# A post-norm decoder layer on one core: x loaded first, weight set-up spread over the first batches, bf16 sums and new step orders

## The chip, the cores and the metric

One core of a Trainium2 chip runs the kernel. The metric is device time in microseconds of one execution. TensorE does matmuls (PE, its weight loads are PEld), VectorE is DVE, ScalarE is ACT, GpSimd is POOL, and SyncE's queue (SP) issues all transfers of this kernel.

## The reference

For each of 64 batches, with 128 tokens of 512 features:

```
qkv = x @ Wqkv; q, k = rmsnorm(q) * w, rmsnorm(k) * w; 16 heads of 32; rope
x = layernorm(x + softmax(causal(q k^T / sqrt(32))) v @ Wo)
# cross step on x and ctx, both cut by tokens into 8 heads of 16 rows:
#   q = x rows (16 x 512), k = v = ctx rows (16 x 512)
#   scores 512 x 512 = q^T k / 4; softmax; out (16 x 512)
x = layernorm(x + cross(x, ctx))
# ffn: x and weight (512 x 512) rounded to fp8 e4m3 in blocks of 128, scaled back
x = layernorm(x + x_deq @ w_deq.T)
```

## The kernel before

All five engines run one software pipeline over the batches. A batch passes through stages 0 to 8; in a slot t an engine works on stage s of batch t − s. Each engine has its list (SP_STEPS, POOL_STEPS, ACT_STEPS, DVE_STEPS, PE_STEPS) of words like `ffn:2@7`: step ffn, part 2, stage 7. It goes through its list in order once per slot, skipping batches that do not exist; slots 0 to 10 are written out, then 25 rounds of two slots are a loop, then the rest is written out. A step waits on semaphores for what it needs, so a step that waits holds all behind it on its engine. The list is cyclic: what counts is the order round the slot. Where it is cut, and so the stage number of a step, only names the turn.

The products are split for accuracy: a value is a high half in f16 and a low half in f16, and a projection of one 128-row part is three matmuls of 128x512 (split); Wo uses fp32r halves (linear).

What passes in one batch:

- SP loads x (ld_x). ACT squares it (x_square), TensorE sums the squares over partitions with a matrix of ones, plus a tiny value (x_sum, two fp32 matmuls of one column), DVE makes a power-of-two scale (x_exp) and from it vinv. POOL and ACT make the halves xs (x_scale, x_high, x_low), SP turns them by a DMA transpose (turn_x).
- TensorE projects q, k, v (proj_q, proj_k, proj_v). q and k go through squares, rms, rope_terms, rope_sum, part_high and part_low, and SP turns each by a DMA transpose (turn_parts:0 and :1, line 414) into qs and ks.
- Self scores come in two turns: self_scores for the maxima (self_max), whose negatives become two more rows of qs by way of DRAM (self_shift, st_sh1, ld_sh1), then self_scores_T, exp (self_probs), mask, self_pv, self_recip, self_norm, oT_high and oT_low, proj_o, add_self, layer norm 0 (layer_mean, layer_devs, layer_rstd, layernorm). x2 is stored.
- The context is loaded (ld_cx, into the one buffer cx, which context_T of the batch before must have read), scaled and split (ctx_square, ctx_sum as x_sum, ctx_exp, context_high, context_low), and turned by TensorE (context_T). q rows and k rows go to DRAM and back in a cross layout (st_qpl, st_kpl, ld_qp, ld_kp).
- 16 cross_scores, each a pair of matmuls on 64-row tiles into the one tile mx, each read by a cross_max on DVE (line 811, 128x1024); then cross_shift, st_sh2, ld_sh2; 16 cross_scores_T into the one tile st, each read by an exp on ACT (probs, line 645) into pp; 8 cross_pv, 32-column tiles; cross_turn, cross_scale, add_cross, layer norm 1.
- The fp8 rounding: quant_scale and quant_magic (DVE), quant_unit and quant_round (POOL), then the halves xd (xd_high, xd_low), their DMA transpose turn_xd (line 465), four ffn parts (line 983), add_ffn, layer norm 2, st_out.

Each full-bank product takes a bank of a fixed three by turn. cross_shift, its rows' store and load must be through before cross_scores_T:0.

Ahead of the lists stands the set-up. SP loads wqkv, wffn, wo and then x's first batch; ACT squares wqkv and wffn; DVE and TensorE make the weight scales (u_wsc); ACT and DVE make w_h and w_l, wo_h and wo_l; then DVE quantises each of the four blocks of the ffn weights, TensorE turns it and DVE splits it (wf_h, wf_l). Only after u_done do ACT, POOL and TensorE go into their lists.

Of the kernel before, what the change touches and what calls it, by code (L numbers as in the profile page):

```python
# [5 lines left out]
def post_ln_decoder_kernel(nc, x, ctx_in, wqkv, q_norm_w, k_norm_w, wo, wffn, cos_t, sin_t, out):  # L6
# [43 lines left out]
    with es:  # L50
# [141 lines left out]
        POOL_STEPS = steps("""  # L192
            ctx_scale:0@4 layer_rstd:0@3 layer_mean:2@8 context_low:0@4 layer_rstd:2@8 layer_mean:1@7
            mean_square:0@1 layer_rstd:1@7 rope_sum:0@1 mean_square:1@1 part_low:0@1 quant_unit:0@7
            mask:0@2 mask:1@2 rope_sum:1@1 mask:2@2 mask:3@2 cross_scale:0@6 quant_round:0@7
            query_low:0@3 part_low:1@1 oT_low:0@2 quant_round:1@7 quant_round:2@7 xd_low:0@7
            x_scale:0@0 x_low:0@0 cross_scale:1@6 layer_mean:0@2""")
        ACT_STEPS = steps("""
            probs:8@6 layernorm:0@3 square:0@1 layer_devs:1@7 probs:9@6 layernorm:1@7 probs:10@6
            square:1@1 part_high:0@1 self_probs:0@2 probs:11@6 query_high:0@3 value:0@1  # L200
            self_probs:1@2 probs:12@6 x_square:0@0 self_probs:2@2 probs:13@6 self_probs:3@2
            part_high:1@1 probs:14@6 probs:15@6 oT_high:0@2 probs:0@5 context_out:0@4 probs:1@5
            ctx_square:0@3 xd_high:0@7 probs:2@5 x_high:0@0 probs:3@5 probs:4@5 layer_devs:0@2
            probs:5@5 context_high:0@3 probs:6@5 layer_devs:2@7 probs:7@5 layernorm:2@7""")
        DVE_STEPS = steps("""
            self_shift:0@2 cross_max:12@5 rope_terms:0@1 cross_max:13@5 quant_scale:0@7
            cross_max:14@5 cross_max:15@5 rope_terms:1@1 cross_shift:0@5 cross_max:0@4 cross_turn:0@6
            cross_max:1@4 quant_magic:0@7 cross_max:2@4 self_recip:0@2 self_norm:0@2 cross_max:3@4
            x_exp:0@0 cross_max:4@4 cross_turn:1@6 cross_max:5@4 add_self:0@2 cross_max:6@4
            self_max:0@1 ctx_exp:0@3 self_max:1@1 cross_max:7@4 self_max:2@1 cross_max:8@4  # L210
            ctx_inv:0@4 add_ffn:0@7 cross_max:9@4 self_max:3@1 cross_max:10@4 add_cross:0@6
            cross_max:11@4""")
        PE_STEPS = steps("""
            cross_scores_T:10@6 proj_k:2@1 proj_k:3@1 cross_scores:14@5 proj_v:0@1 proj_v:1@1
            self_scores_T:0@2 cross_scores_T:11@6 cross_scores:15@5 proj_v:2@1 proj_v:3@1
            self_scores_T:1@2 cross_scores_T:12@6 cross_scores:0@4 cross_pv:3@6 self_pv:0@2
            self_scores_T:2@2 cross_scores_T:13@6 self_pv:1@2 cross_scores:1@4 self_scores_T:3@2
            cross_pv:4@6 self_pv:2@2 cross_scores:2@4 cross_scores_T:14@6 self_pv:3@2 cross_pv:5@6
            cross_scores_T:15@6 cross_scores:3@4 cross_pv:6@6 context_T:0@4 cross_scores_T:0@5
            x_sum:0@0 cross_pv:7@6 cross_scores:4@4 cross_scores_T:1@5 proj_o:0@2 proj_o:1@2  # L220
            cross_scores:5@4 cross_scores_T:2@5 proj_o:2@2 proj_o:3@2 cross_scores:6@4
            cross_scores_T:3@5 self_scores:0@1 self_scores:1@1 ctx_sum:0@3 cross_pv:0@5
            cross_scores:7@4 cross_scores_T:4@5 self_scores:2@1 ffn:0@7 ffn:1@7 cross_scores_T:5@5
            cross_scores:8@4 ffn:2@7 ffn:3@7 cross_scores_T:6@5 cross_scores:9@4 proj_q:0@0
            self_scores:3@1 cross_scores_T:7@5 cross_scores:10@4 proj_q:1@0 proj_q:2@0
            cross_scores_T:8@5 cross_scores:11@4 proj_q:3@0 proj_k:0@0 proj_k:1@0 cross_scores:12@4
            cross_scores_T:9@5 cross_pv:1@5 cross_pv:2@5 cross_scores:13@4""")
# [924 lines left out]
```

## Time and profile before

| | |
|---|---|
| median of 3 runs | 2737.21 us (2735.64 to 2741.36) |
| profiled execution, its time | 2741.84 us |
| its span, first to last instruction | 2740.1 us |
| mean granted TensorE clock | 0.971 |
| busy: PE, DVE, ACT, POOL | 91%, 80%, 76%, 61% |
| chain that ended last: PE, SP queue, DMA | 65%, 11%, 9% |

Starts and durations in a timeline are in us from the span's start. PE durations overlap, since matmuls are pipelined; the distance from one start to the next is the price.

### The profile page before, as it was taken

The numbers are of one execution on the slowest core, as the hardware profiler recorded it, in microseconds if no ns is written. First come the engines' busy times: TensorE is split into PE (matmuls) and PEld (weight loads), VectorE is DVE, ScalarE is ACT, GpSimd is POOL, SyncE is SP. The second block draws the span as 40 slices with busy tenths as digits, with TensorE's granted clock in tenths as the row PEclk, the third lists the DMA queues.
The fourth block names the chain that finished last, engine by engine and source line by source line (L and its number), as shares of the span: only waits on it lengthen the run. The fifth ranks groups of instructions, "written<-read, shape, count | busy, mean of one in ns | idle before, by whom it ended". The sixth has DMA issues, their size and how long they took to land.

```text
span 2740.1 us, 67073 instructions
## 1 busy us (share of the span) xinstructions
PE 2488.1 (91%) x19220; PEld 992.2 (36%) x19220; DVE 2203.3 (80%) x3525; ACT 2074.7 (76%) x3097; POOL 1670.0 (61%) x2586
## 2 busy tenths in 40 slices
PE   0679999999999999999999999999999999998874
PEld 0333333343334333333333333433333333433211
...
GB/s 88 66 103 121 119 125 114 129 123 121 119 129 119 128 112 131 121 128 112 127 128 125 115 119 132 123 118 122 128 119 123 117 131 120 130 115 115 71 41 28
DMA packets 610637, 312.01 MB, mean 114 GB/s; under 512 B 469504, under 2 KB 551424, under 8 KB 610560
## 3 DMA queue, kind: packets, MB, share of 16 engines
...
q8 instruction: 39, 0.64, 0.1%
q14 instruction: 38, 0.31, 0.0%
...
## 4 chain that ended last, share of the span: by engine, by line
PE 65%; SPq 11%; DMA 9%; issue 5%; DVE 5%; POOL 3%; ACT 2%; ACTq 0%; POOLq 0%; DVEq 0%
PE bank L983 25%; PE pv L1112 13%; PE mx L1085 8%; PE st L1099 7%; DMA xdT<-xd 7%; SPq L414 5%; PE bank L1048 2%; PE bank L1030 2%; PE bank L975 2%; PE bank L1051 2%; DVE nm L811 2%; SPq L388 2%; SPq L398 1%; PE bank L968 1%; SPq L379 1%
## 5 line engine op out<-in xcount | busy, mean ns | idle before, releaser
L811 DVE TENSOR_REDUCE nm<-mx 128x2 f32<-128x1024 f32 x1024 | 1248.5, 1219 | 248.7 <-PE mx L1085 241.9
L645 ACT ACTIVATE pp<-st,esc 128x1024 f32<-128x1024 f32 x1024 | 1139.3, 1113 | 341.8 <-PE st L1099 339.1
L1112 PE MATMUL pv<-pp,vT 128*32 128x512 f32 x4096 | 550.3, 622 | 1.2 <-DVE o2t L906 0.9
L983 PE MATMUL bank<-w_h,xsT 128*128 128x512 f16 x1536 | 525.0, 384 | 9.3 <-DMA xsT<-xs 6.3
L1085 PE MATMUL mx<-kp,qp 48*128 48x512 f16 x2048 | 400.7, 388 | 36.9 <-DVE nm L811 34.4
L1099 PE MATMUL st<-qp,kp 50*128 50x512 f16 x2048 | 401.2, 388 | 25.0 <-ACT pp L645 25.0
L983 PE MATMUL bank<-w_l,xsT 128*128 128x512 f16 x768 | 293.0, 381 | 0.0
L983 PE MATMUL bank<-wf_h,xdT 128*128 128x512 f16 x512 | 180.2, 394 | 83.2 <-DMA xdT<-xd 83.1
L983 PEld LDWEIGHTS bank<-w_h,xsT 128*128 128x128 f16 x1536 | 150.1, 98 | 278.2 <-issue 131.1
L534 POOL TENSOR_SCALAR neg_mean<-total 128x1 f32<-128x1 f32 x192 | 36.5, 190 | 329.3 <-DVE yout L938 207.2
L558 POOL TENSOR_SCALAR_AFFINE_SELECT p<-p 128x512 f32<-128x512 f32 x256 | 168.3, 657 | 108.1 <-ACT p L695 103.1
L1085 PEld LDWEIGHTS mx<-kp,qp 48*128 48x128 f16 x2048 | 99.4, 94 | 354.9 <-DVE nm L811 229.4
L872 DVE SCALAR_TENSOR_TENSOR rope<-bank,rms,rope_w 128x1024 f32<-128x1024 f32 x128 | 163.4, 1277 | 37.6 <-POOL rms L514 19.9
L841 DVE TENSOR_REDUCE nm<-bank 128x4 f32<-128x512 f32 x256 | 174.6, 683 | 14.9 <-PE bank L1020 14.9
L1099 PEld LDWEIGHTS st<-qp,kp 50*128 50x128 f16 x2048 | 99.5, 94 | 219.4 <-ACT pp L645 120.9
L695 ACT ACTIVATE p<-bank 128x512 f32<-128x512 f32 x256 | 156.1, 610 | 24.2 <-PE bank L1030 24.1
L511 POOL TENSOR_SCALAR rms<-ssq,xeps 128x1 f32<-128x1 f32 x128 | 33.9, 265 | 192.6 <-ACT junk L669 192.4
L552 POOL TENSOR_TENSOR qkn<-rope,qkn 128x512 f16<-128x512 f32 x128 | 148.0, 1156 | 3.2 <-ACT qkn L676 3.2
L1112 PEld LDWEIGHTS pv<-pp,vT 128*32 128x32 f32 x4096 | 93.6, 110 | 141.4 <-issue 131.8
L711 ACT ACTIVATE x<-x,shift,rstd 128x512 f32<-128x512 f32 x128 | 103.3, 807 | 48.5 <-POOL shift L543 48.5
L975 PE MATMUL bank<-wo_h,oT_h 128*128 128x512 f32 x256 | 116.7, 456 | 6.6 <-POOL oT_l L574 6.6
L539 POOL TENSOR_SCALAR rstd<-devs 128x1 f32<-128x1 f32 x192 | 36.6, 190 | 133.6 <-ACT junkd L706 123.2
...
## 6 DMA issues: line engine op xcount, KB each, us to landing
qp<-q_rows SPq DMA_DIRECT2D x256, 96.0 KB, 2.3
kp<-k_rows SPq DMA_DIRECT2D x256, 96.0 KB, 2.2
...
```

Source lines behind the costliest of these rows:

```text
L552: g_.tensor_tensor(qkn[k][:, :, 2 - k, :], rope[:, 0].rearrange("p h a d -> p h (a d)"), qkn[k][:, :, 0, :], ALU.subtract).then_inc(s_part ...
L558: g_.affine_select(out=p1[c % 2][:], in_=p1[c % 2][:], compare_op=ALU.is_ge, fill=0.0, base=0, pattern=[[0, HC], [1, P]], channel_multipli ...
L645: a.activation(pp[:, unit % PB, 2 * l:2 * (l + 1), :], st[:], ACT.Exp, scale=esc[b.i][:])\
L695: a.activation(p1[c % 2][:], at(f"s1t{c}")[:].rearrange("p (h q) -> p h q", h=HC), ACT.Exp, scale=SELF_SCALE).then_inc(bank_free[BANK[f"s1 ...
L811: v.tensor_reduce(cols, mx[:], AX.X, ALU.max, negate=True).then_inc(mx_free, 1)
L841: v.tensor_reduce(nm1[:, HC * c:HC * (c + 1)], at(f"s1m{c}")[:].rearrange("p (h k) -> p h k", h=HC), AX.X, ALU.max, negate=True).then_inc( ...
L872: v.scalar_tensor_tensor(rope[:].rearrange("p t h a d -> p t (h a d)"), at("qk"[k])[:].unsqueeze(1).to_broadcast([P, 2, D]), rms[:, k:k + ...
L975: last = t.matmul(at(name)[:], a[:, rows], w[:, part, cols], start=(part == 0 and i == 0), stop=(part == KC - 1 and i == 2))
L983: last = t.matmul(at(name)[:], lin[:, KC * lo + part, :], w[:, part, cols], start=(part == 0 and i == 0), stop=(part == KC - 1 and i == 2))
L1085: last = t.matmul(mx[:, q, :], qp[b.i][rows, p, c * P:(c + 1) * P], kp[b.i][rows, p, :], start=True, stop=True)
L1099: last = t.matmul(st[:, q, :], kp[b.i][rows, p, i * P:(i + 1) * P], qp[b.i][rows, p, :], start=True, stop=True)
L1112: last = t.matmul(pv[32 * j:32 * j + 2 * XD, :], vT[b.i][:, i, GROUPS * j + g, :], pp[:, unit % PB, j, :], start=(i == 0), stop=(i == KC - 1))
```

## The change

- **Set-up.** ld_x of batch 0 goes first on SP, then the loads of wqkv and wffn. Functions of the set-up are hooked ahead of or behind steps of given batches (ahead, behind in run): qkv_high, qkv_low and qkv_scale make the q, k, v weights after the first x_high, x_exp and ahead of the first proj_q; fixed_rows (POOL's memsets of qkn, vT and kp) after the weight scale; load_wo, wo_high, wo_low ahead of turn_parts:0, self_probs:0, self_recip of batch 0; wf_halves(0) ahead of the first self_max, (1) to (3) ahead of add_self of batches 0, 1, 2.
- **ffn weights.** wf_halves writes the halves of a block into xd, and SP turns it by a DMA transpose (turn_wf) into wf; the ffn matmuls read their moving operand as four pieces of 128 columns.
- **Sums.** ones and tiny are bf16; x_sum, ctx_sum and the weights' sum read the upper 16 bits of the fp32 squares as bf16.
- **Small moves.** xeps goes from x_scale to behind x_low; vinv from x_exp to behind rope_terms:0.
- **Orders.** All five lists are new; the steps are the same.

```diff
         SP_STEPS = steps("""
-            ld_kp:1@5 st_qpl:0@4 ld_qp:1@5 turn_xd:0@8 turn_x:0@1 ld_x2r:0@7 ld_qp:0@4 ld_x:0@0
-            st_out:0@8 st_sh1:0@2 st_kpl:0@4 ld_sh1:0@2 ld_kp:0@4 st_sh2:0@5 st_x2:0@3 ld_xr:0@2
-            ld_sh2:0@5 turn_parts:0@1 ld_cx:0@3 turn_parts:1@1""")
+            st_sh2:0@5 ld_x:0@0 ld_sh2:0@5 turn_parts:0@1 turn_parts:1@1 ld_qp:1@4 ld_kp:1@4
+            ld_cx:0@3 turn_xd:0@7 st_qpl:0@3 turn_x:0@0 ld_x2r:0@6 ld_qp:0@3 st_kpl:0@3 st_sh1:0@1
+            st_out:0@7 ld_sh1:0@1 ld_kp:0@3 st_x2:0@2 ld_xr:0@1""")
         POOL_STEPS = steps("""
...
+            context_low:0@4 layer_mean:0@3 layer_mean:2@8 cross_scale:1@7 layer_rstd:2@8
+            layer_rstd:0@3 mean_square:0@1 layer_mean:1@7 layer_rstd:1@7 rope_sum:0@1 mean_square:1@1
+            mask:0@2 part_low:0@1 mask:1@2 quant_unit:0@7 rope_sum:1@1 mask:2@2 mask:3@2 part_low:1@1
+            quant_round:0@7 quant_round:1@7 oT_low:0@2 quant_round:2@7 xd_low:0@7 x_scale:0@0
+            cross_scale:0@6 query_low:0@3 x_low:0@0 ctx_scale:0@3""")
         DVE_STEPS = steps("""
...
+            add_self:0@3 self_max:1@2 cross_max:7@5 ctx_exp:0@4 cross_max:8@5 self_max:2@2
+            cross_max:9@5 add_ffn:0@8 self_max:3@2 cross_max:10@5 self_shift:0@2 cross_max:11@5
+            add_cross:0@7 cross_max:12@5 rope_terms:0@1 cross_max:13@5 cross_max:14@5 quant_scale:0@7
+            ctx_inv:0@5 cross_max:15@5 cross_shift:0@5 cross_max:0@4 rope_terms:1@1 cross_max:1@4
+            cross_turn:0@6 quant_magic:0@7 cross_max:2@4 self_recip:0@2 self_norm:0@2 cross_max:3@4
+            x_exp:0@0 cross_max:4@4 cross_max:5@4 cross_turn:1@6 cross_max:6@4 self_max:0@1""")
         PE_STEPS = steps("""
...
+            cross_scores_T:10@6 cross_scores:12@5 proj_k:0@1 cross_pv:1@6 cross_pv:2@6
+            cross_scores:13@5 proj_k:1@1 proj_k:2@1 cross_scores_T:11@6 cross_scores:14@5 proj_k:3@1
+            self_scores_T:0@2 proj_v:0@1 cross_scores_T:12@6 cross_scores:15@5 proj_v:1@1 proj_v:2@1
+            cross_scores_T:13@6 cross_scores:0@4 self_scores_T:1@2 proj_v:3@1 cross_pv:3@6
+            cross_scores_T:14@6 cross_scores:1@4 self_pv:0@2 self_scores_T:2@2 self_pv:1@2
+            cross_scores_T:15@6 self_scores_T:3@2 cross_scores:2@4 cross_pv:4@6 self_pv:2@2
+            self_pv:3@2 cross_pv:5@6 cross_scores_T:0@5 cross_scores:3@4 cross_pv:6@6 x_sum:0@0
+            cross_scores_T:1@5 cross_pv:7@6 cross_scores:4@4 cross_scores_T:2@5 context_T:0@4
+            proj_o:0@2 cross_scores:5@4 cross_scores_T:3@5 proj_o:1@2 proj_o:2@2 cross_scores:6@4
+            cross_scores_T:4@5 self_scores:0@1 proj_o:3@2 self_scores:1@1 cross_scores_T:5@5
+            cross_scores:7@4 cross_pv:0@5 ctx_sum:0@3 ffn:0@7 cross_scores_T:6@5 cross_scores:8@4
+            ffn:1@7 self_scores:2@1 cross_scores_T:7@5 cross_scores:9@4 ffn:2@7 ffn:3@7
+            self_scores:3@1 cross_scores_T:8@5 cross_scores:10@4 proj_q:0@0 proj_q:1@0
+            cross_scores_T:9@5 cross_scores:11@4 proj_q:2@0 proj_q:3@0""")
...
+            def load_weights():
+                for c in range(KC):
+                    sp.dma_start(pp[:, c].rearrange("p a d -> p (a d)")[:, 0:3 * D], wqkv[c * P:(c + 1) * P, :])\
+                      .then_inc(d_setup[c], 16)
+                for c in range(KC):
+                    sp.dma_start(wf_rows[c][:], wffn[c * P:(c + 1) * P, :]).then_inc(d_wffn, 16)
...
+            def turn_wf(c):
+                sp.wait_ge(u_wf, c + 1)
+                sp.dma_start_transpose(wf[:, c], xd[:].rearrange("p a d -> p (a d)")).then_inc(d_wf, 16)
...
+            def fixed_rows():
+                pool.wait_ge(u_wsc, 1)
+                for n, (rows, value) in enumerate([(qkn[0][:, :, 3, :], 0.0), (qkn[1][:, :, 3, :], SHIFT_UNIT)] + [
+                        (vT[i][:, :, :, XD:2 * XD], 1.0) for i in range(2)] + [
+                        (kp[i][ROW_TILE * q + 32:ROW_TILE * (q + 1), :, :], SHIFT_UNIT) for i in range(2) for q in range(2)]):
+                    pool.wait_ge(u_const, U_FIRST + n)
+                    g_.memset(rows, value).then_inc(u_const, 1)
+                pool.wait_ge(u_const, U_CONST)
...
+            def wf_halves(c):
+                y3 = yq[:].rearrange("p (n k) -> p n k", n=NQ)
                 src = wf_rows[c][:].rearrange("p (n k) -> p n k", n=NQ)
...
+                if c:
+                    dve.wait_ge(d_wf, 16 * c)
+                step(v.tensor_copy(xd[:, 0, :], yq[:]))
+                v.tensor_tensor(xd[:, 1, :], yq[:], xd[:, 0, :], ALU.subtract).then_inc(u_wf, 1)
...
-                t.matmul(at("xt")[:, 0:1], ones[:], xss[:], start=True, stop=False)
-                t.matmul(at("xt")[:, 0:1], ones[:], tiny[:], start=False, stop=True).then_inc(bank_full[BANK["xt"]], 1)
+                t.matmul(at("xt")[:, 0:1], ones[:], xss[:].bitcast(BF16)[:, 1:2], start=True, stop=False)
+                t.matmul(at("xt")[:, 0:1], ones[:], tiny[:, 0:1], start=False, stop=True).then_inc(bank_full[BANK["xt"]], 1)
...
-                split("ffn", xdT, wf_h, wf_l, slice(0, D), part)
+                for i, (lo, w_lo) in enumerate(((0, 0), (0, 1), (1, 0))):
+                    last = t.matmul(at("ffn")[:].rearrange("p (c n) -> p c n", c=KC), xdT[:, KC * lo + part, :],
+                                    wf[:, :, KC * w_lo + part, :], start=(part == 0 and i == 0),
+                                    stop=(part == KC - 1 and i == 2))
```

The four old lists besides SP's are the kernel's own above. POOL's ended `... rope_sum:1@1 mask:2@2 mask:3@2 cross_scale:0@6 quant_round:0@7 query_low:0@3 part_low:1@1 oT_low:0@2 quant_round:1@7 quant_round:2@7 xd_low:0@7 ...`, and DVE's had cross_max:14 and :15 side by side and no other two.

## Rows read from the trace of the kernel before

**Rows 1.** Windows: length, busy time (instructions) per engine, PEclk, DMA share, GB/s.

```profile
0.00:75.15 75.15, 6.43 (x24) 4.72 (x25) 38.71 (x72) 20.09 (x28) 13.66 (x29) 1.00 0.24 85
75.15:301.00 225.85, 181.98 (x1343) 85.81 (x1345) 134.08 (x212) 116.34 (x197) 114.08 (x172) 0.91 0.44 101
...
600.00:2152.00 1552.00, 1510.17 (x11978) 607.76 (x11976) 1347.84 (x2160) 1280.15 (x1920) 1034.62 (x1599) 1.00 0.49 123
```

**Rows 2.** The line of the v scale, batches 8 to 63 (window 300 to 2600 us).

```profile
L866 DVE TENSOR_SCALAR vinv<-sx,wtop x56: 212/214/215, 326.5 to 2467.1; 128x1 int32<-128x1 int32 x56
```

**Rows 3.** Timeline of the set-up: start, duration, instruction, [idle before <- releaser].

```profile
3.58 7.37 POOL L497 MEMSET kp<- 32x2048 f16 x4
...
10.31 0.42 DVE L761 SCALAR_TENSOR_TENSOR rope_w<-rope,sin_s 128x256 f32<-128x256 f32 x1
...
24.52 7.00 DVE L777 SCALAR_TENSOR_TENSOR w_l<-pp,wsc,w_h 128x1536 f16<-128x1536 f32 x4 [1.64 <-ACT w_h L634]
...
35.48 0.68 DVE L789 TENSOR_REDUCE amax<-x 128x4 f32<-128x512 f32 x1
...
39.97 0.69 DVE L798 TENSOR_TENSOR yq<-yq,qsc 128x512 f32<-128x512 f32 x1
...
67.01 0.63 ACT L658 ACTIVATE junkx<-xb 128x512 bf16<-128x512 f32 x1 [32.18 <-DVE amax L805]
...
75.15 0.61 PE L983 MATMUL bank<-w_h,xsT 128*128 128x512 f16 x1 [6.33 <-DMA xsT<-xs]
```

**Rows 4.** Waits from 600 to 2152 us: us in total, times, longest.

```profile
PE bank L983 <- DMA xdT<-xd: 40.4, 40, 1.5
...
DVE nm L811 <- PE mx L1085: 124.2, 120, 2.2
```

**Rows 5.** Chain of waits, one batch: start, duration, piece.

```profile
1300.60 0.60 PE bank L968 x4
...
1302.13 3.06 SPq L414
...
1309.17 3.38 DMA xdT<-xd
```

**Rows 6.** Timeline of POOL and of SP's queue in that batch.

```profile
1306.23 1.16 POOL L603 TENSOR_TENSOR xd<-yq,xd 128x512 f16<-128x512 f32 x1 [0.88 <-ACT xd L732]
...
1295.58 2.92 SPq L443 DMA_DIRECT2D qp<-cross_shift  x4
```

**Rows 7.** Timeline of TensorE in that batch.

```profile
1277.05 0.38 PE L1085 MATMUL mx<-kp,qp 48*128 48x512 f16 x2
1277.36 0.39 PE L983 MATMUL bank<-w_h,xsT 128*128 128x512 f16 x1
...
1301.43 0.38 PE L991 MATMUL bank<-xss,ones 128*128 128x1 f32 x2
...
1301.97 1.06 PE L1112 MATMUL pv<-pp,vT 128*32 128x512 f32 x8
...
1308.23 0.38 PE L1017 MATMUL bank<-maskb,identb 128*128 128x512 bf16 x1
1308.45 0.39 PE L1020 MATMUL bank<-ks,qs 96*128 96x128 f16 x4
1308.67 0.34 PE L1073 MATMUL bank<-css,ones 128*128 128x1 f32 x2
...
1309.16 1.06 PE L1112 MATMUL pv<-pp,vT 128*32 128x512 f32 x8
```

**Rows 8.** A group of lines (busy, mean ns), then DVE's timeline in that batch.

```profile
L1017 PEld LDWEIGHTS bank<-maskb,identb 128*128 128x128 bf16 x256 | 24.9, 97 | 71.1 <-issue 61.3 <-DVE nm L841 1.8 <-DVE cbits L827 0.9
...
1290.22 1.23 DVE L811 TENSOR_REDUCE nm<-mx 128x2 f32<-128x1024 f32 x1 [0.64 <-PE mx L1085]
...
1293.08 0.24 DVE L822 STREAM_TRANSPOSE sh2T<-sh 128x64 f16<-128x64 f16 x1
```

**Rows 9.** Waits from 75 to 290 us: us in total, times, longest.

```profile
DVE x L899 <- PE bank L975: 15.0, 5, 6.7
```

**Rows 10.** Timeline of DVE in the fill.

```profile
98.33 0.69 DVE L841 TENSOR_REDUCE nm<-bank 128x4 f32<-128x512 f32 x1 [9.00 <-PE bank L1020]
```

More of the change, by code:

```diff
@@ L192, in post_ln_decoder_kernel @@
         POOL_STEPS = steps("""
[L193 to L197, printed above, removed]
-        ACT_STEPS = steps("""
[L199 to L204, printed above, removed]
@@ L205, in post_ln_decoder_kernel @@
-        DVE_STEPS = steps("""
[L206 to L212, printed above, removed]
@@ L213, in post_ln_decoder_kernel @@
-        PE_STEPS = steps("""
[L214 to L227, printed above, removed]
@@ L309, in last_of, with run @@
                     for i in sorted({p.bank for p in points})]
-        def run(eng, table, fns):
+        def run(eng, table, fns, ahead, behind):
             def slot(t, rnd=None):
@@ L315, in slot @@
                     if 0 <= t - stage < BATCH:
+                        if (name, k, t) in begins:
+                            ahead[begins[name, k, t]]()
                         fns[name](Count(t - stage, rnd), k)
+                        if (name, k, t) in ends:
+                            behind[ends[name, k, t]]()
+            stage_of = {(name, k): stage for name, k, stage in table}
+            begins = {(name, k, stage_of[name, k] + b): (name, k, b) for name, k, b in ahead}
+            ends = {(name, k, stage_of[name, k] + b): (name, k, b) for name, k, b in behind}
             for t in range(LOOP0):
@@ L492, in _ @@
             n = 4
[L493 to L495 removed]
+            for rows, value in [(ones[:], 1.0), (tiny[:], TINY), (sums_of[:], 0.0)]:
                 pool.wait_ge(u_const, n)
@@ L614, in _ @@
                 "part_low": part_low, "mask": mask,
-                "context_low": context_low, "xd_low": xd_low, "cross_scale": cross_scale, "oT_low": oT_low, "quant_unit": quant_unit, "quant_round": quant_round, "query_low": query_low})
+                "context_low": context_low, "xd_low": xd_low, "cross_scale": cross_scale, "oT_low": oT_low, "quant_unit": quant_unit, "quant_round": quant_round, "query_low": query_low},
+                ahead={("mean_square", 0, 0): fixed_rows}, behind={})
         @block.scalar
@@ L947, in _ @@
                 "cross_turn": cross_turn, "add_cross": add_cross, "quant_scale": quant_scale,
-                "quant_magic": quant_magic, "add_ffn": add_ffn})
+                "quant_magic": quant_magic, "add_ffn": add_ffn}, ahead={
+                    ("self_max", 0, 0): lambda: wf_halves(0), ("self_recip", 0, 0): wo_low,
+                    ("add_self", 0, 0): lambda: wf_halves(1), ("add_self", 0, 1): lambda: wf_halves(2),
+                    ("add_self", 0, 2): lambda: wf_halves(3)},
+                behind={("x_exp", 0, 0): qkv_low})
         @block.tensor
@@ L1126, in _ @@
                 "cross_scores": cross_scores, "ctx_sum": ctx_sum,
-                "cross_scores_T": cross_scores_T, "cross_pv": cross_pv, "ffn": ffn})
+                "cross_scores_T": cross_scores_T, "cross_pv": cross_pv, "ffn": ffn}, ahead={
+                    ("proj_q", 0, 0): qkv_scale, ("proj_o", 0, 0): wo_ready, ("ffn", 0, 0): wf_ready}, behind={})
 def kernel(x, ctx_2048, L0_attn_Wqkv, L0_attn_q_norm_w, L0_attn_k_norm_w, L0_attn_Wo, L0_ffn_weight):
```

183 lines of the change are left out of this document (94 added, 89 removed).

## The prediction

> **What bounds the kernel now.** I read the windows by stage first [rows 1]. There the reader is to see the stages. In the first 75 us TensorE does 6.4 us of work while DVE sets up weights. From 75 to 301 us the pipeline fills. Between 600 and 2152 us everything repeats: by the first and last of the rows of the v scale [rows 2] batches 8 to 63 follow one another every (2467.1 − 326.5)/55 = 38.92 us, and the forty batches of the 1552 us window every 38.8 us. After the last v scale at 2467 the pipeline drains for 273 us.
>
> Set-up next [rows 3]. The q, k, v weights are ready when DVE's four w_l passes end, at 31.5 us. After that DVE quantises and turns the ffn weights, four rounds of about 7.85 us (35.48 to 67.0), and only then may ACT square the first x (idle before it 32.2 us) and the first projection start, at 75.15. Nothing in the first projection needs the ffn weights: 75.15 − 31.5 = 43.6 us is order alone.
>
> In the steady state TensorE is busy 1510 of 1552 us, and the waits there [rows 4] have one entry for its matmuls: the turned xd, 40.4 us in 40 times, 1.0 us a batch. The DVE waits for scores, 124.2/40 = 3.1 us a batch, are idle time of an engine that has some. The chain [rows 5] shows why xdT is late. It leaves TensorE at the context transpose (1300.60), goes to the SP queue, where the load of cx waited for it, then through the 3.06 us that turning k holds the queue, two kp loads, the q stores, two qp loads, and issues the transpose of xd at 1309.17, 8.0 us after the context was turned; it lands 3.38 us later and ffn starts. xd itself was complete on POOL at 1306.23 + 1.16 = 1307.39 [rows 6]: the queue, not the data, was last, by 1.8 us. So a batch costs 37.8 us of TensorE's own order and 1.0 us for the SP queue's order.
>
> **The change, part by part.** *Sums over partitions.* The two fp32 matmuls on the squares of x and the two on those of the context take 1301.97 − 1301.43 = 0.54 us and 1309.16 − 1308.67 = 0.49 us [rows 7], 1.03 us a batch, each fp32 matmul being two instructions (x2 in the rows). In bf16 they are four instructions with a load of 97 ns (24.9 us in 256, [rows 8]). The bound below is the pitch of the 128-column f16 matmuls, 128x512 columns' worth in 0.22 us for four (1308.45 to 1308.67), so 0.22 for the four together; the bound above is half of today's, 0.52, since half the instructions go. I take 0.42, close to four loads of 97 ns, because a one-column matmul can hide no load: 0.6 us saved a batch, 0.5 to 0.8.
>
> The row of bf16 loads stands at 97 ns [rows 8]. [...]
>
> *New order on TensorE.* The same 75 steps. Inside a run of full-array matmuls the pitch is 0.22 us; where the order goes over to the 64-row pairs of the cross scores and back it is 0.31 (1277.05 to 1277.36) [rows 7]: a change of tile shape costs 0.09 us. Counted round the list, the order before has 41 such changes, the new one 42: +0.1 us. The Trainium skill says on the page "TensorEngine Tiling (Array Packing)", section "Key Properties", that changing the tiling mode drains the engine; it names no price, and by its rule too the new order is the dearer one, by one drain. The trace agrees and prices it.
>
> *New order on SP.* ld_cx is now followed at once by turn_xd; turn_parts:1 and the loads of the second halves stand ahead of ld_cx, the q store and loads behind. From the end of context_T the path to ffn is now the issue of cx, which took less than 0.9 us with its semaphores (1301.20 to 1302.13, rows 5), and a 3.4 us transpose, some 4.3 us. Adding up the TensorE steps between context_T and ffn:0 in the new list (four proj_o at 0.71, two self_scores at 0.44, six cross steps at 0.22, one cross_pv at 0.88, the sum, nine shape changes) gives 6.8 us. That link has 2.5 us to spare; before it was 11.4 against some 10. What is late next: POOL's xd_low. Its new list puts query_low and cross_scale:0 (each about as long as the 1.16 us of xd_low or less) behind xd_low and lets nothing new in front, so against the scores it ends about 1 to 2 us sooner than the 1307.39 of today, which was already early. After that come the two transposes of q and k, now back to back. The second must leave the queue (3.06 us), then four loads (0.4 us each at the transfers' pace of rows 6) and ld_cx, before turn_xd; laid beside the TensorE list, part_low:1 ends about 7.8 us after cross_scores:0, so turn_xd goes at about 14 to 15, lands at 17.4 to 18.5, and ffn:0 stands at 18.9. Room of 0.4 to 1.5 us: I cost the wait at 0, with 1.0 as its other end.
>
> *New orders on DVE, ACT, POOL.* DVE is busy 33.7 us of 38.8 (1347.84/40, rows 1). A cross_max can't start before its scores and the next scores not before it ends, so where two stand side by side DVE idles 0.64 us (1290.22, [rows 8]). The new list has two such pairs for one of before, and x_exp gives up the 0.3 us of vinv. DVE then needs some 35.5 us of a batch; a batch of 37.3 still covers it, but with 1.8 us to spare instead of 3.3. Before moves nothing for it. The mean bound: TensorE loses 0 to 0.6 us a batch where a cross_max is late.
>
> So a batch goes from 38.8 to 38.8 − 1.0 − 0.6 + 0.1 = 37.3 us, and over 55 batches that is 55 × 1.5 = 82 us (bounds 36.9 and 38.2: 104 and 33 us).
>
> *Set-up.* SP loads x first (under 0.5 us of queue), then the weights. ACT squares x, and DVE's x_exp comes behind its rope tables, which end at about 10.7; x_high ends about 1 us later [rows 3]. ACT then starts the squares of the weights some 2 us later than before, of which most was waiting for data; with the queue's 0.5 I take 0.8 us for the whole chain: the weight scale, known 1.64 us before the first w_l at 24.52, comes at 23.7, and w_l ends near 32.3. POOL's four memsets of kp (7.37 us) and the four smaller ones (an eighth to a quarter of its data each, taken as 2.2 in all) are moved behind the weight scale: they end at 33.3, and TensorE, ACT and SP all wait for them. First projection at about 33.5 instead of 75.15: 41.7 us saved. Bounds: 38 (everything of x in line with the weights' squares, 2 us more, and slower loads) and 43.6.
>
> *What set-up costs later.* Each of the four wf_halves is the DVE round of before, 5.2 us from 35.48 to 39.97 + 0.69 [rows 3], plus a copy and a subtraction of 0.69 each, 6.6 us in all; their transposes go by SP, half as many columns each as that of k. wo adds four passes at 0.69 on DVE and as many on ACT. That is 29 us of DVE in the fill, where it is busy 134 of 226 us [rows 1]. The first round stands before the first self_max, where DVE idled 9.0 us for the turned k (98.33, [rows 10]): hidden. The others stand before add_self, where DVE idled 15.0 us in 5 times, 3 us each [rows 9]: 6.6 − 3 = 3.6 us late, three times. Taken as all exposed with wo it would be 3 × 6.6 + 5 = 25 us, and 0 if the slots are bound elsewhere. I take 8. The ffn matmuls read the weights in four pieces of 128 columns at a stride; the nearest row, the mask matmul with its repeated 128-column piece, keeps the full pitch (1308.23 to 1308.45), so 0. The drain keeps its steps: 0, within ±8.
>
> **The sum.** The profiled execution took 2741.84 us (span 2740.1 and 1.7 around it). 2741.84 − 41.7 + 8 − 82 = 2626. The median of the runs is 4.6 us below that execution, so 2621; I say 2620.
>
> **The rivals.** *A, as summed: 2620*, its own range 2590 to 2650. *B, the SP queue or POOL still brings xdT last.* For it: the two transposes stand together, and the room is only 0.4 to 1.5 us. Against it: the 8.0 us between context and issue falls to about 0.7. Then only the sums' 0.5 us remains: 2737 − 34 − 28 = 2675, and with nothing left of it 2703. *C, DVE takes the bound.* For it: 35.5 of 37.3 us and two adjacent pairs. Period 37.9: 2737 − 34 − 50 = 2653. *D, slower: the shift rows come too late for cross_scores_T:0.* In the trace sh2T is made at 1293.08 [rows 8] and the last of four issues on SP is out at 1298.5 [rows 6]; even if it lands 2 us after its start that is about 6.7 us after the shift; the new list gives 7.6 us from the shift to cross_scores_T:0. DVE would have to run more than 0.9 us late for any wait; it decides at a wait of 1.5 + 34/55 = 2.1 us a batch, that is with cross_shift 3 us late. At 2.5 us a batch the time is 2737 − 34 + 55 = 2758. Against it: DVE had 3.3 us of idle time a batch for its waits [rows 4], and catches up. *E, better: 2575*, TensorE's sums at 0.22 us and small waits gone too (period 36.6).
>
> **How the numbers follow.** A 0.50, B 0.22, C 0.13, D 0.05, E 0.10. The range 2585 to 2695 leaves out half of E (0.05), a third of B (0.07) and D (0.05). A measurement of this kernel can tell about 0.2%, 5.5 us. Faster 0.94 (all but D and a sliver), same 0.01, slower 0.05.
>
> **What would show it.** First projection near 33.5 us; no DVE round of the ffn weights ahead of it. Batches 8 to 63 at 37.3 us by the rows of vinv. No entry of TensorE for xdT in the steady waits; bf16 rows of the sums with two instructions a step. DVE busy about 33.7 of 37.3. B shows as an xdT wait with SP's turn_parts in the chain, C as cross score matmuls waiting for nm, D as st matmuls waiting for cross_shift. A first projection later than 45 us, a period above 38.2, or a fill (first projection to batch 8) longer by more than 25 us than 251 us would prove the sum wrong.

## The result and the profile after

The changed kernel takes **2624.08 us** (median of 3 runs, 2621.92 to 2624.45) where the kernel before takes 2737.21: a ratio of 0.9582, with a 95% interval of 0.956 to 0.9603. The forecast was 2620, the range 2585 to 2695. The profiled execution took 2624.45 us with a span of 2622.7. Its page, busy time and the chain that ended last:

```profile
PE 2448.5 (93%) x18946; PEld 932.2 (36%) x18946; DVE 2204.5 (84%) x3524; ACT 2096.8 (80%) x3097; POOL 1686.3 (64%) x2586
...
PE 87%; DVE 4%; issue 2%; POOL 2%; ACT 2%; DMA 2%; SPq 0%; POOLq 0%; DVEq 0%; ACTq 0%
```

In the kernel before, TensorE had 65% of the chain and SP's queue 11%; now TensorE has 87% and the queue nothing. The windows of the fill and of the steady state (columns as in [rows 1]):

```profile
33.00:260.00 227.00, 160.01 (x1067) 72.03 (x1070) 136.37 (x222) 94.05 (x163) 93.65 (x139) 0.81 0.41 93
600.00:2152.00 1552.00, 1551.86 (x12361) 596.47 (x12360) 1407.71 (x2251) 1351.21 (x2000) 1089.16 (x1663) 1.00 0.51 128
```

TensorE is busy 1551.86 of 1552 us (its ends are modelled), where it was 1510.17 [rows 1], and its list of waits from 600 to 2152 us is empty: the 40.4 us for xdT [rows 4] have no successor. DVE still waits for scores, though less than the 124.2 us of [rows 4]:

```profile
DVE nm L842 <- PE mx L1126: 90.0, 168, 0.7
```

DVE needs 1407.71/1552 of the time, 33.8 us of a batch of 37.2.

To divide the gain I take one marker in both traces, the transpose sh2T on DVE, once a batch. Before: batch 8 at 516.54 us, then 38.906 us a batch. After, batches 8 and 63:

```profile
492.61 0.24 DVE L853 STREAM_TRANSPOSE sh2T<-sh 128x64 f16<-128x64 f16 x1
...
2540.09 0.24 DVE L853 STREAM_TRANSPOSE sh2T<-sh 128x64 f16<-128x64 f16 x1
```

That is (2540.09 − 492.61)/55 = 37.227 us a batch. The difference of the spans, 2740.1 − 2622.7 = 117.4 us, splits so:

| part | before | after | gained |
|---|---|---|---|
| first projection at | 75.15 | 32.88 | 42.3 |
| from there to sh2T of batch 8 | 441.4 | 459.7 | −18.3 |
| 55 batches at | 38.906 | 37.227 | 92.4 |
| from sh2T of batch 63 to the end | 83.7 | 82.6 | 1.1 |

The 38.906 holds two long intervals where the drain begins, 40.65 and 43.83 us, with the granted clock at 0.89 and 0.81 (windows between the rows of sh2T):

```profile
2495.50:2536.15 40.65, 32.98 (x260) 12.17 (x260) 31.86 (x49) 29.13 (x39) 20.21 (x31) 0.89 0.45 106
2536.15:2579.98 43.83, 33.93 (x232) 11.10 (x226) 28.77 (x42) 26.33 (x34) 15.91 (x25) 0.81 0.28 73
```

Batches 8 to 58 alone follow every 38.82 us before and every 37.23 after. The changed kernel has no interval above 38.4 us.

Three more places of the after trace. **Set-up**: ACT and DVE, then POOL and TensorE (timeline as in [rows 3]):

```profile
8.67 0.63 ACT L691 ACTIVATE junkx<-xb 128x512 bf16<-128x512 f32 x1 [6.51 <-DMA xb<-x]
...
24.46 7.01 DVE L812 SCALAR_TENSOR_TENSOR w_l<-pp,wsc,w_h 128x1536 f16<-128x1536 f32 x4 [1.73 <-ACT w_h L662]
...
25.45 7.37 POOL L529 MEMSET kp<- 32x2048 f16 x4
...
32.88 0.61 PE L1024 MATMUL bank<-w_h,xsT 128*128 128x512 f16 x1 [10.91 <-POOL kp L529]
```

The projection starts 0.06 us after the memsets of kp end (25.45 + 7.37 = 32.82); the w_l passes end at 31.47, so the memsets are last by 1.35 us.

**SP's queue** in one steady batch (timeline: start, duration of the issue), and xd on POOL. xd_low ends at 1289.08 and its transpose is issued at 1289.25, so SP now waits for the data. xdT lands at 1292.31 and ffn starts at 1293.34, 1.0 us later:

```profile
1287.30 0.36 SPq L384 DMA_DIRECT2D cx<-ctx  x1
1289.25 1.24 SPq L483 DMA_TRANSPOSE xdT<-xd  x1
...
1287.92 1.16 POOL L632 TENSOR_TENSOR xd<-yq,xd 128x512 f16<-128x512 f32 x1 [0.88 <-ACT xd L767]
```

**TensorE** at the two sums of that batch (compare 1301.43 and 1308.67 in [rows 7]):

```profile
1283.95 0.18 PE L1032 MATMUL bank<-xss,ones 128*128 128x1 bf16 x1
1283.99 0.16 PE L1033 MATMUL bank<-tiny,ones 128*128 128x1 bf16 x1
1284.10 0.39 PE L1140 MATMUL st<-qp,kp 50*128 50x512 f16 x2
...
1293.27 0.18 PE L1114 MATMUL bank<-css,ones 128*128 128x1 bf16 x1
1293.31 0.16 PE L1115 MATMUL bank<-tiny,ones 128*128 128x1 bf16 x1
1293.34 0.81 PE L1162 MATMUL bank<-wf,xdT 128*128 128x512 f16 x3
```

From the start of a sum to the next matmul it is 0.15 us with a change of tile shape and 0.07 us without one: 0.22 us a batch, where the four fp32 matmuls took 1.03. The two are not quite alike, since before a change of tile shape stood behind both sums; e4 below, with the new order and fp32, makes them alike.

### The profile page after: what moved, and what is told of

Its sections match the earlier page's. It is cut to its first block, busy times and chain, and to the rows that moved or that the text cites. A ratio compares the mean times of both kernels' runs of the same rounds, so it can differ in the third digit from the quotient of the medians.

```text
span 2622.7 us, 66428 instructions
## 1 busy us (share of the span) xinstructions
PE 2448.5 (93%) x18946; PEld 932.2 (36%) x18946; DVE 2204.5 (84%) x3524; ACT 2096.8 (80%) x3097; POOL 1686.3 (64%) x2586
## 4 chain that ended last, share of the span: by engine, by line
PE 87%; DVE 4%; issue 2%; POOL 2%; ACT 2%; DMA 2%; SPq 0%; POOLq 0%; DVEq 0%; ACTq 0%
PE bank L1024 19%; PE pv L1153 18%; PE st L1140 11%; PE mx L1126 10%; PE bank L1016 7%; PE bank L1162 7%; PE bank L1089 3%; PE bank L1071 3%; PE bank L1058 2%; PE bank L1061 2%; PE bank L1092 2%; DVE nm L842 1%; PE bank L1009 1%; ACT pp L678 1%; DMA xdT<-xd 0%
## 5 line engine op out<-in xcount | busy, mean ns | idle before, releaser
L1024 PE MATMUL bank<-w_h,xsT 128*128 128x512 f16 x1536 | 547.2, 386 | 12.9 <-POOL kp L529 10.9
L1153 PE MATMUL pv<-pp,vT 128*32 128x512 f32 x4096 | 544.6, 617 | 0.4 <-DVE o2t L938 0.3
L1024 PEld LDWEIGHTS bank<-w_h,xsT 128*128 128x128 f16 x1536 | 150.6, 98 | 266.4 <-issue 132.0
L1162 PE MATMUL bank<-wf,xdT 128*128 128x512 f16 x768 | 203.2, 389 | 23.5 <-DMA xdT<-xd 23.4
L587 POOL TENSOR_SCALAR_AFFINE_SELECT p<-p 128x512 f32<-128x512 f32 x256 | 183.2, 726 | 39.0 <-ACT p L728 38.9
L899 DVE SCALAR_TENSOR_TENSOR rope<-bank,rms,rope_w 128x1024 f32<-128x1024 f32 x128 | 163.7, 1279 | 44.2 <-POOL rms L541 23.5
L702 ACT ACTIVATE junk<-bank 128x512 bf16<-128x512 f32 x128 | 76.4, 597 | 86.6 <-PE bank L1024 77.0
L593 POOL TENSOR_SCALAR cxs<-cx,sc 128x512 f32<-128x512 f32 x64 | 44.2, 690 | 136.0 <-DVE sc L862 136.0
L739 ACT ACTIVATE junkd<-x,neg_mean 128x512 bf16<-128x512 f32 x128 | 92.4, 722 | 48.0 <-POOL neg_mean L563 42.0
```

The lines of the kernel that those rows point to most:

```text
L587: g_.affine_select(out=p1[c % 2][:], in_=p1[c % 2][:], compare_op=ALU.is_ge, fill=0.0, base=0, pattern=[[0, HC], [1, P]], channel_multipli ...
L899: v.scalar_tensor_tensor(rope[:].rearrange("p t h a d -> p t (h a d)"), at("qk"[k])[:].unsqueeze(1).to_broadcast([P, 2, D]), rms[:, k:k + ...
L1024: last = t.matmul(at(name)[:], lin[:, KC * lo + part, :], w[:, part, cols], start=(part == 0 and i == 0), stop=(part == KC - 1 and i == 2))
L1153: last = t.matmul(pv[32 * j:32 * j + 2 * XD, :], vT[b.i][:, i, GROUPS * j + g, :], pp[:, unit % PB, j, :], start=(i == 0), stop=(i == KC - 1))
L1162: last = t.matmul(at("ffn")[:].rearrange("p (c n) -> p c n", c=KC), xdT[:, KC * lo + part, :], wf[:, :, KC * w_lo + part, :], start=(part ...
```

## The experiments

Eleven runs. Each ratio is to the kernel before, run again on the same chip: e1 to e4 on one chip, e5 to e8 on a second, e9 to e11 on a third. The medians of the kernel before on these three are 2732.04, 2732.51 and 2739.17 us, so times of different chips can't be compared to better than 0.3%. "us a batch" is between the sh2T of batches 8 and 63, "fill" from the first projection to the sh2T of batch 0. The last four columns are of one profiled execution each, and the fills of one kernel differ by 3 us (160.9 and 157.8).

| run | median us | ratio, 95% | first projection | fill | us a batch | span |
|---|---|---|---|---|---|---|
| kernel before | 2737.21 | 1 | 75.15 | 129.0 | 38.906 | 2740.1 |
| changed | 2624.08 | 0.9582 | 32.88 | 160.9 | 37.227 | 2622.7 |
| e1 bf16 sums only | 2753.69 | 1.0087 [1.006, 1.0114] | 73.68 | 131.1 | 39.03 | 2751.1 |
| e2 turn_xd earlier | 2701.97 | 0.9889 [0.9862, 0.9917] | 75.04 | 131.2 | 38.321 | 2701.4 |
| e3 both | 2697.66 | 0.9878 [0.9853, 0.9903] | 73.49 | 129.0 | 38.194 | 2694.2 |
| e4 orders only | 2684.14 | 0.9824 [0.9799, 0.9849] | 75.07 | 132.0 | 38.021 | 2682.3 |
| e5 old orders | 2722.51 | 0.9965 [0.9948, 0.9982] | 33.01 | 140.4 | 39.194 | 2725.5 |
| e6 rounds elsewhere | 2611.36 | 0.9561 [0.9545, 0.9577] | 32.82 | 147.9 | 37.216 | 2606.0 |
| e7 fewer shape changes | 2673.57 | 0.9788 [0.9771, 0.9806] | 32.8 | 157.2 | 38.116 | 2671.7 |
| e8 e6, e7, wo moved | 2663.65 | 0.9752 [0.9736, 0.9769] | 32.83 | 147.0 | 38.088 | 2661.6 |
| e9 rounds one slot earlier | 2607.88 | 0.9516 [0.95, 0.9532] | 32.8 | 144.9 | 37.28 | 2608.3 |
| e10 e1 with needless matmuls | 2732.63 | 0.9974 [0.996, 0.9987] | 73.58 | 128.9 | 38.789 | 2730.9 |
| e11 changed kernel again | 2623.64 | 0.9578 [0.9562, 0.9594] | 32.78 | 157.8 | 37.282 | 2620.9 |

**e1: the bf16 sums alone.** The kernel before with `ones` and `tiny` in bf16 and the high halves of the sums as operands:

```
-t.matmul(at("xt")[:, 0:1], ones[:], xss[:], start=True, stop=False)
-t.matmul(at("xt")[:, 0:1], ones[:], tiny[:], start=False, stop=True)
+t.matmul(at("xt")[:, 0:1], ones[:], xss[:].bitcast(BF16)[:, 1:2], start=True, stop=False)
+t.matmul(at("xt")[:, 0:1], ones[:], tiny[:, 0:1], start=False, stop=True)
```

> Before, with the sums over partitions in bf16 and nothing else. Additive theory (my sum): TensorE's own order gets 0.6 to 0.9 us shorter, so a batch falls from 38.9 to about 38.1 and the time by 40 to 55 us, to about 2690. Rival (the queue theory taken to its end): both sums stand between context_T and ffn in TensorE's list, and that stretch is waited out by the SP queue's path from context_T to the turned xd; then the batch stays at 38.9, the wait for xdT grows from 1.0 to about 1.8 us, and the time stays within 5 us of before.

It became 0.9% slower, which neither the sum nor the rival had. In this order both sums lie between the context transpose and ffn, inside the stretch that SP's queue waits out [rows 5], so what TensorE saves it waits. Waits of TensorE from 600 to 2152 us, against 40.4 in [rows 4]:

```profile
PE bank L984 <- DMA xdT<-xd: 67.3, 40, 2.3
```

That explains no gain, but not a loss. The loss is uneven: of the 55 batches, 10 take over 40 us, while the median batch is 38.7 us, a little below the 38.9 of before. Nine of the ten lie before the drain, where the kernel before has none. The windows of one of the ten (columns as in [rows 1], PEclk the third from the end) and its timeline on TensorE:

```profile
1355.00:1360.00 5.00, 3.65 (x34) 1.49 (x33) 4.73 (x9) 3.48 (x6) 3.85 (x7) 1.00 0.75 198
1360.00:1365.00 5.00, 4.39 (x14) 1.28 (x15) 1.07 (x2) 1.25 (x3) 0.93 (x3) 0.66 0.28 52
1365.00:1370.00 5.00, 4.97 (x30) 1.69 (x29) 4.74 (x8) 4.13 (x7) 2.24 (x5) 1.00 0.31 87
```

```profile
1360.61 0.45 PE L984 MATMUL bank<-wf_h,xdT 128*128 128x512 f16 x1 [1.96 <-DMA xdT<-xd]
1360.86 0.63 PE L984 MATMUL bank<-wf_l,xdT 128*128 128x512 f16 x1
1361.29 1.06 PE L984 MATMUL bank<-wf_h,xdT 128*128 128x512 f16 x2
...
1364.58 0.59 PE L984 MATMUL bank<-wf_h,xdT 128*128 128x512 f16 x2
1365.01 0.38 PE L984 MATMUL bank<-wf_l,xdT 128*128 128x512 f16 x1
```

After a wait of 1.96 us the granted clock is at its lower level, 1.2 GHz, and the matmuls follow one another every 0.43 us (1360.86 to 1361.29) and not every 0.22 us (two from 1364.58 to 1365.01), until about 1364.1. 3.5 us of work at half the pace cost some 1.7 us beside the wait itself. Each of the nine holds one such stretch at the lower clock, and no other batch from 8 to 58 does. But not every wait of that length is followed by one: of the 24 waits of 1.68 us and more between 500 and 2500 us, nine are and fifteen are not, the longest among them:

```profile
1048.00:1053.00 5.00, 4.97 (x28) 1.86 (x28) 2.71 (x5) 2.92 (x4) 0.81 (x4) 1.00 0.21 39
```

```profile
1048.03 0.39 PE L984 MATMUL bank<-wf_h,xdT 128*128 128x512 f16 x1 [2.28 <-DMA xdT<-xd]
```

No run here shows what decides between the two.

**e10: the same wait filled with work.** e1, with needless work: four mask matmuls into the ffn bank, which ffn then overwrites, ahead of the wait for xdT; the wait for the ffn bank moves ahead of them.

```
+for _ in range(4):
+    t.matmul(at("ffn")[:].rearrange("p (h k) -> p h k", h=HC), identb[:],
+             maskb[:].unsqueeze(1).to_broadcast([P, HC, P]), start=True, stop=True)
 pe.wait_ge(d_xdT, b.n(16, 16))
```

> e1 (before with bf16 sums) with four needless 128x512 matmuls into the ffn bank while TensorE waits for xdT; their result is overwritten. Clock theory (e1 is slower because waits of about 2 us bring the granted clock down to 1.2 GHz for the matmuls behind them, in one batch of four): the work fills 0.9 us of each 1.7 us wait, the slots of 40.7 us go, all take 38.5, and more work gives less time: 2720 to 2730, at or under before. Rival (e1's batches are longer for another reason): no change, about 2753, or longer by up to 55 us.

More work, less time: 0.9974 of before against e1's 1.0087, and 2732.63 us against 2753.69, though on two chips (1.1% by the ratios, 0.8% by the times). One batch of 55 is over 40 us, in the drain, and the median is 38.8; the wait for xdT is 27.5 us in 37 times, longest 1.6, and no batch from 8 to 58 has a stretch at the lower clock. The idle time made the loss, through the clock. The Trainium skill, page "TensorE: Matmul & The Clock Gate", section "What's actually happening", gives the array 1.2 GHz when idle and 2.4 GHz when busy. The rows of e1 agree on the two levels, 0.43 and 0.22 us a matmul; here the lower one came behind a wait of 1.96 us in a stream that was otherwise busy.

**e2 and e3: the queue alone, then with the sums.** One step moved in SP's list; e3 is e1 with that.

```
-ld_kp:1@5 st_qpl:0@4 ld_qp:1@5 turn_xd:0@8 turn_x:0@1
+ld_kp:1@5 turn_xd:0@8 st_qpl:0@4 ld_qp:1@5 turn_x:0@1
```

> Before, with only turn_xd moved in SP's list ahead of the q store and the second q loads (behind ld_kp:1). Queue theory: the issue comes about 1.7 us sooner, right after xd is complete, xdT is there in time, the 1.0 us wait a batch goes, a batch takes 37.9, the time falls by about 60 us to 2677. Rival (xdT's wait only covers another wait, of DVE or POOL, that comes last next): the batch falls by less than 0.4 us and the time by less than 25.

> Before, with turn_xd moved as in e2 and the sums in bf16 as in e1. Queue theory: once the queue is not last, the sums count: 0.6 to 0.9 us a batch less than e2, a batch of 37.1 to 37.3, time about 2630. Rival: the sums never counted, e3 equals e2.

e2 shows the queue to be the cause of the wait: moving one issue takes the xdT wait away and 38.906 − 38.321 = 0.59 us a batch with it. It isn't the full 1.0, in part because the q store and loads it jumped are now late themselves (11.9 us in 40 batches, 0.3 us a batch; 0.1 isn't accounted for). TensorE's waits from 600 to 2152 us in e2, then in e3:

```profile
PE mx L1085 <- DMA qp<-q_rows: 11.9, 35, 0.6
```

```profile
PE mx L1086 <- DMA qp<-q_rows: 28.1, 41, 0.9
PE bank L984 <- DMA xdT<-xd: 1.4, 8, 0.2
```

So in e3, forecast at about 2630 us, the sums' 0.8 us brought only 0.13 us a batch: 0.4 went to a longer wait for q, and some 0.25 isn't accounted for.

**e4 and e5: orders without the rest, the rest without the orders.** e4 is the kernel before with the five new lists; e5 the changed kernel with the five old ones.

> Before, with the five new lists and nothing else (old set-up, fp32 sums, vinv and xeps where they were). My sum: 38.9 - 1.0 + 0.1 = 38.0 a batch, time about 2680. If the orders give more than their wait for xdT (small waits that no row of mine showed), a batch is below 37.8. The first projection stays at 75 us, and since no ffn weight round stands in the fill, the fill from the first projection to the first cross_shift is as long as before (129 us) if the longer fill of the changed kernel comes from the rounds, and about 30 us longer if it comes from the orders.

> The changed kernel with the five old lists: new set-up, bf16 sums, old orders. Theory (the parts add, and the rounds of the ffn weights cost their whole length in the fill): first projection at 33, but the fill to the first cross_shift about 30 us longer than the 131 us of e1, batches as in e1 at 39.0 to 39.1; so 10 us less than e1, about 2743, not faster than before. Rival (the set-up's 42 us stay): 2711.

e4 has 38.021 us a batch and no wait of TensorE: 0.885 less than before. Of that 0.79 is left over batches 8 to 58 (38.82 to 38.03), beside the long intervals of before: near the 1.0 us wait less 0.1 us for one more shape change, with another 0.1 open. From e4 to the changed kernel it is 38.021 − 37.227 = 0.79 us. In one order the sums save as much: in e4 they take 0.54 and 0.47 us up to the next matmul, in the changed kernel 0.15 and 0.07.

```profile
1315.98 0.38 PE L990 MATMUL bank<-xss,ones 128*128 128x1 f32 x2
...
1316.52 0.39 PE L1098 MATMUL st<-qp,kp 50*128 50x512 f16 x2
...
1325.70 0.38 PE L1072 MATMUL bank<-css,ones 128*128 128x1 f32 x2
...
1326.17 0.38 PE L982 MATMUL bank<-wf_h,xdT 128*128 128x512 f16 x1
```

The ffn's operand in four pieces and the small moves lie between e4 and the changed kernel too; no run takes them apart, and the 0.79 leaves nothing for them. e4's fill is 132.0 us, 3.0 longer than before, so the orders don't by themselves explain the 31.9 of the changed kernel.

e5, at 2722.51 us, lies between the 2743 of its theory and the 2711 of its rival. It has the wait of e1 back, 66.4 us in 39 times, and 39.19 us a batch. Its fill is 9.3 us longer than e1's (140.4 against 131.1): the same rounds cost less there than under the new orders. By spans, the orders alone gain 57.8 us, the rest alone 14.6, both 117.4, so 45 us come from the two together. In the 55 batches it is 59.5 us: under the old orders the rest loses 0.29 us a batch and under the new ones it gains 0.79. Up to batch 8 it is 14.9 us the other way: there the rest costs 459.7 − 432.9 = 26.8 us under the new orders and 453.3 − 441.4 = 11.9 under the old.

**e6, e9 and e11: where the rounds stand.** First DVE in the fill of the changed kernel (timeline):

```profile
90.33 0.69 DVE L872 TENSOR_REDUCE nm<-bank 128x4 f32<-128x512 f32 x1 [6.69 <-PE bank L1061]
90.94 0.67 DVE L824 TENSOR_REDUCE amax<-x 128x4 f32<-128x512 f32 x1
...
96.61 0.69 DVE L837 TENSOR_TENSOR xd<-yq,xd 128x512 f16<-128x512 f32 x1
97.22 0.68 DVE L931 SCALAR_TENSOR_TENSOR x<-bank,xr 128x512 f32<-128x512 f32 x1
```

and who waits for the step behind the round (waits from 33 to 260 us):

```profile
PE bank L1114 <- DVE x L931: 13.4, 2, 6.8
...
PE bank L1058 <- DVE x L931: 6.5, 1, 6.5
```

The round takes 97.22 − 90.94 = 6.3 us and DVE has no idle time ahead of L931 to give up for it: the idle time, 6.69 us, lies one step earlier, ahead of self_max:0. L931 is late by the whole round, and TensorE waits for it three times, once for each round, 19.9 us in all. e6 moves the three rounds into that gap:

```
-("add_self", 0, 0): lambda: wf_halves(1), ("add_self", 0, 1): lambda: wf_halves(2),
-("add_self", 0, 2): lambda: wf_halves(3)},
+("self_max", 0, 1): lambda: wf_halves(1), ("self_max", 0, 2): lambda: wf_halves(2),
+("self_max", 0, 3): lambda: wf_halves(3)},
```

> The changed kernel with wf_halves(1), (2), (3) ahead of self_max:0 of batches 1, 2, 3 instead of ahead of add_self of batches 0, 1, 2, one step sooner on DVE. Theory: there DVE idles 6.7 to 6.8 us for the first self scores while nothing waits for it, and a round takes 6.3 us, so three rounds leave the path: the fill falls from 161 to about 142 us, the time to about 2605; the batches stay at 37.24. Rival (the fill is long by the SP queue's transposes or by the order, not by the rounds): less than 5 us.

The fill falls from 160.9 to 147.9 us (142 forecast), TensorE's waits for L931 from 19.9 to 11.7 us, and the steady state stays (37.216). e9 takes each round an idle place earlier, and puts their transposes on SP ahead of turn_parts:0 of batches 1 to 3; e11 is the changed kernel once more on the same chip.

```
+("rope_terms", 0, 1): lambda: wf_halves(1), ("self_max", 0, 1): lambda: wf_halves(2),
+("self_max", 0, 2): lambda: wf_halves(3)},
```

> The changed kernel with the ffn weight rounds in DVE's gaps of slots 2 and 3: wf_halves(1) ahead of rope_terms:0 of batch 1 (gap 5.6 us), (2) and (3) ahead of self_max:0 of batches 1 and 2 (gaps 6.7 us), their transposes ahead of turn_parts:0 of batches 1, 2, 3. Theory: e6 left one round exposed, in slot 4 where the cross scores begin (44 us against 38 in e4); it goes, so 5 to 6 us less than e6, a fill of 142 us, 0.9535 of before. Rival (slot 4 is long for another reason, or a transpose of the weights ahead of that of q holds q up): no less than e6.

> The changed kernel again, as the measure for e9 on the same chip: 0.958 of before.

e9 takes 2607.88 us and e11 2623.64, 0.6% more; the intervals of their ratios don't touch. The fill is 144.9 against 157.8, TensorE waits 4.9 us for L931, and sh2T of batch 8 stands at 476.57 − 32.8 = 443.8 us behind the first projection, against 456.5 in e11: place is worth 12.7 us. What is left isn't nothing. The 443.8 are only 2.4 more than before, but the new orders without the set-up's work reach batch 8 in 432.9 (e4), so 10.9 us and what the cheaper sums save up to there are still paid. e6 and e9 weren't run on one chip: the times (2607.74 to 2612.52 and 2605.34 to 2610.01) overlap, the ratios (0.9561 and 0.9516) don't, so which is faster stays open. Both beat the kernel before and the changed one.

**e7 and e8: fewer changes of tile shape.** Two steps of TensorE's list moved, 39 changes a batch for 42:

```
-cross_scores_T:15@6 self_scores_T:3@2 cross_scores:2@4 ... cross_pv:6@6 x_sum:0@0
-cross_scores_T:1@5 cross_pv:7@6 cross_scores:4@4
+self_scores_T:3@2 cross_scores_T:15@6 cross_scores:2@4 ... cross_pv:6@6 cross_pv:7@6
+x_sum:0@0 cross_scores_T:1@5 cross_scores:4@4
```

> The changed kernel with two moves in TensorE's list: self_scores_T:3 ahead of cross_scores_T:15, and cross_pv:7 right behind cross_pv:6. The order then has 39 changes of tile shape in place of 42. Theory (TensorE is full, and each change costs 0.09 us of it): 0.27 us a batch less, 36.97, and 17 us less in all, about 2607. Rival (the gaps at the changes are waits for other engines or DVE and ACT are last by now): within 5 us of 2624, or slower where cross_scores_T:1 now comes too late for ACT.

> The changed kernel with e6 and e7 together, and wo_high ahead of square:0 of batch 1 and wo_low ahead of rope_terms:0 of batch 1, where ACT idles 14.6 us and DVE 5.6 us. Theory: 19 us of e6, 17 us of e7 and some 3 us more, about 2585; first projection at 33, fill about 139 us, batches at 36.97. Rival: the two gains don't add, because a shorter fill only brings the next wait forward.

e7, forecast at about 2607 us, lost 0.89 us a batch instead, as the last words of its rival had it. The three changes gave nothing that can be seen, since a wait came in; TensorE's waits from 600 to 2152 us:

```profile
PE st L1140 <- ACT pp L678: 40.8, 41, 1.0
PE bank L1071 <- ACT p L728: 8.0, 41, 0.2
```

and the chain of waits, one batch:

```profile
1302.84 0.34 PE st L1140 x2
1303.20 1.12 ACT pp L678
1304.33 0.05 issue
1304.37 0.39 PE st L1140 x2
```

cross_scores_T:2 needs the buffer st that ACT's exponential of cross_scores_T:1 must first read, 1.12 us. In the changed kernel cross_pv:7 stood between the two. Waits of 1.0 + 0.2 us less the 0.89 lost leave 0.3 us, 0.1 for each change removed; that is a remainder and not a measurement of its own. e8 (2585 forecast, with e7's gain in it) adds e6 and the wo passes in earlier places: 38.088 us a batch as in e7, a fill of 147.0 where e6 has 147.9. The parts add up here, since they lie in different stages.

## Why the forecast held, step by step

*Set-up: right.* 33.5 us was forecast for the first projection, 32.88 measured; the memsets of kp end last, as the step had it, and the w_l passes end at 31.47 us for the 32.3 forecast.

*xdT: right.* The wait is gone, and e2 shows by one moved issue that SP's queue made it. Rival B, the queue still last, didn't happen: each turn_parts issue takes 2.0 us in the steady batch where 3.06 was assumed from one batch (the median before is 2.1, from 600 to 2152 us), and the transpose waits for POOL, with 1.0 us of room behind it. (The path from 1301.20 to 1302.13 that the sum calls less than 0.9 us is 0.93; nothing hangs on it.)

*Sums: right in kind, mis-sized.* 0.42 us for four was assumed, since a one-column matmul can hide no load of 97 ns. That reason was wrong: the two sums take 0.15 and 0.07 us up to the next matmul, 0.22 in all, though the load rows still last 95 to 99 ns each (medians). The saving is 0.8 us and not 0.6. The Trainium skill, page "TensorE: Matmul & The Clock Gate", section "Weight-path perf modes — Fast Weight Load (FWL) and DoubleRow", gives about 2× as measured for such loads on trn2. An estimate from that and the 97 ns rows is 0.05 us a load, 0.2 us for four and 0.8 us saved, as measured; no run here shows whether that is the reason.

*Shape changes: not contradicted.* +0.1 us for one more was forecast. e4's period, 38.02, is what 38.906 − 1.0 + 0.1 gives, but over batches 8 to 58 the same sum gives 37.9 and e4 has 38.03; no run isolates a single change.

*Period: 37.3 forecast, 37.23 measured.* It also fell from a higher base, 38.906 over batches 8 to 63 and not 38.8, so the 55 batches gave 92.4 us and not 82. The two long intervals at the start of the drain are that difference in base, some 6 us; the sum had none of it.

*DVE: right.* It needs 33.8 us of 37.2 and TensorE never waits for it in the steady state; C and D didn't happen. E's period, 36.6, wasn't reached either. (E's sum is off: 2737 − 34 − 55 × 2.2 is 2582, and 2575 only with nothing for what set-up costs later.)

*What set-up costs later: the step that was mis-sized.* "6.6 − 3 = 3.6 us late, three times", 8 us in all, where the way up to batch 8 grew by 18.3 us (15.1 in e11). Two things in it failed. First, 3 us was the mean of five waits before L899 [rows 9]. In the kernel before they are 6.45, 6.74 and 0.62 us ahead of add_self of batches 0, 1 and 2:

```profile
125.31 0.69 DVE L899 SCALAR_TENSOR_TENSOR x<-bank,xr 128x512 f32<-128x512 f32 x1 [6.45 <-PE bank L975]
...
152.30 0.69 DVE L899 SCALAR_TENSOR_TENSOR x<-bank,xr 128x512 f32<-128x512 f32 x1 [6.74 <-PE bank L975]
...
180.32 0.69 DVE L899 SCALAR_TENSOR_TENSOR x<-bank,xr 128x512 f32<-128x512 f32 x1 [0.62 <-PE bank L975]
```

Under these old orders two of the three rounds have their place, and e5's fill grows by 9.3 us only. The new order puts self_max:0 just ahead of add_self, and the idle time goes there. e4, which has the new orders and no rounds, shows it:

```profile
127.72 0.69 DVE L840 TENSOR_REDUCE nm<-bank 128x4 f32<-128x512 f32 x1 [6.74 <-PE bank L1019]
128.69 0.69 DVE L898 SCALAR_TENSOR_TENSOR x<-bank,xr 128x512 f32<-128x512 f32 x1 [0.28 <-PE bank L974]
```

So in the changed kernel each round is exposed in full, 6.3 us, and TensorE waits 19.9 us for the three; e6 and e9 move them and the waits go down to 11.7 and 4.9.

Second, the 18.3 us are net of a gain that the sum put at nothing: the new orders shorten the fill's later batches too. e4 reaches batch 8 in 432.9 us, 8.5 less than before, so the new set-up with the cheaper sums costs 26.8 us there and not 18.3 (23.6 in e11), and more by what the sums save up to there. The 18.3 lies inside the bounds of 0 to 25; the work itself, at 26.8 in one execution, 23.6 in the other and more without the sums, lies at or above the bound that stood for all exposed. The rounds' 19.9 are most of it. The rest, which holds wo's passes, isn't taken apart. It has the clock in it: from the first projection to the sh2T of batch 0 the granted clock is 0.84 in e4, 0.78 in e11 and 0.76 in the changed kernel, with TensorE busy for 95.2, 96.7 and 101.0 us.

In the sum, 18 for 8 and 92 for 82 cancel, and 42.3 and 1.1 stand for 41.7 and 0. The 4.6 us between the profiled execution and the median of before had no counterpart after (0.4), so the medians differ by 113.1 us and the spans by 117.4. That 2620 came within 5 us of 2624.08 is luck in part: the terms were further off than their sum.
